# A graph layer with attention, mixer and feed-forward: the one-hots of a lot by four VectorE operations, and ScalarE's weights of a lot ahead of its copy of a finished block

## What is computed

```
xn = layernorm(x)
Wh = xn @ W.T + b                          # 4 heads of 64
e  = leaky_relu(a_src(Wh)[i] + a_dst(Wh)[j], 0.2)
out[i] = sum_j softmax_i(e) * Wh[j]        # the graph part: a sum over the edges of node i
x  = x + out + mix(xn)                     # linear attention, two layer norms, an MLP
x  = x + ffn(layernorm(x))                 # shared MLP and the best 2 of 4 experts
```

## Time and profile before

| | |
|---|---|
| median of 3 runs | 3117.58 us (3114.31 to 3119.29) |
| profiled execution: its own time | 3118.8 us |
| profiled execution: span | 3117.0 us |
| mean granted TensorE clock | 0.847 |
| TensorE busy | 2181.7 us (70%) |
| GpSimd busy | 2160.0 us (69%) |
| VectorE busy | 1882.2 us (60%) |
| ScalarE busy | 792.2 us (25%) |

### The profile page before, as it was taken

How to read it: one execution, slowest core, us unless ns; L and a number is a source line. 1 busy time by engine, 2 the same in 40 slices (tenths; PEclk the granted TensorE clock), 3 DMA queues, 4 the chain that set the end, 5 groups by cost and what they waited for, 6 DMA issues and landing times.

```text
span 3117.0 us, 40701 instructions
## 1 busy us (share of the span) xinstructions
PE 2181.7 (70%) x10817; PEld 1529.3 (49%) x10818; DVE 1882.2 (60%) x3946; ACT 792.2 (25%) x1396; POOL 2160.0 (69%) x2141
## 2 busy tenths in 40 slices
PE   1001984177778787787977879778778787787877
PEld 0000552155555555555655556555555555555554
DVE  8998552265664656666566664656655656666463
ACT  6000442022222222222222222222222222222222
POOL 1008777677777777777777777777777777777770
PEclk6555997588989988989889898889989988989988
DMA  6000221434344444444444444444444444444462
GB/s 188 0 0 13 75 74 41 96 101 119 96 103 124 102 111 116 104 123 103 115 110 104 122 102 124 102 103 123 102 106 124 102 117 108 105 123 103 123 91 29
DMA packets 271584, 306.05 MB, mean 98 GB/s; under 512 B 164258, under 2 KB 210856, under 8 KB 271080
## 3 DMA queue, kind: packets, MB, share of 16 engines
q0 software_dynamic: 97760, 251.60, 30.9%
q1 hardware_dynamic: 140098, 18.08, 3.9%
q10 hardware_dynamic: 33480, 33.36, 3.4%
HBM read 276.25 MB, written 26.62 MB: 97 GB/s over the span
## 4 chain that ended last, share of the span: by engine, by line
PE 50%; DVE 14%; issue 8%; POOL 6%; ACT 2%; DMA 1%; ACTq 0%; DVEq 0%; POOLq 0%; SPq 0%; another core or an unknown queue 0%
PE sum_banks L1027 26%; PE f_banks L1042 9%; POOL gathered L965 6%; DVE onehot L1430 5%; PE turned L999 3%; PE f_banks L1161 2%; DVE gathered L1451 2%; PE f_banks L1086 1%; PE sum_banks L1015 1%; PE f_banks L1067 1%; PE f_banks L1162 1%; DVE he L1579 1%; DVE he L1582 1%; PE f_banks L1068 1%; ACT onehot_t L1202 1%
## 5 line engine op out<-in xcount | busy, mean ns | idle before, releaser
L965 POOL DMA_INDIRECT gathered<-table,col x1872 | 1898.4, 1014 | 572.9 <-issue 563.2
L1027 PE MATMUL sum_banks<-gathered,onehot 128*128 128x260 f32 x3744 | 1070.5, 449 | 105.7 <-DVE gathered L1451 104.4
L1027 PEld LDWEIGHTS sum_banks<-gathered,onehot 128*128 128x128 f32 x3744 | 824.8, 226 | 298.1 <-issue 133.0
L1451 DVE TENSOR_TENSOR gathered<-gathered 128x512 f32<-128x512 f32 x936 | 591.4, 692 | 50.6 <-ACT gathered L1206 47.8
L1430 DVE TENSOR_TENSOR onehot<-iota_row,col 128x1024 f32<-128x1024 f32 x236 | 288.9, 1225 | 448.4 <-PE sum_banks L1027 448.0
L290 POOL DMA_INDIRECT edge_list<-payload,pos x244 | 249.9, 1024 | 293.4 <-DVE pos L411 216.5
L1202 ACT COPY onehot_t<-turned 128x1024 bf16<-128x1024 bf16 x236 | 238.6, 1011 | 332.5 <-PE turned L999 330.2
L1216 ACT COPY acc<-sum_banks x234 | 87.8, 375 | 915.4 <-PE sum_banks L1027 700.0
L999 PE MATMUL turned<-ident_bf,onehot 128*128 128x128 bf16 x1888 | 157.7, 231 | 165.6 <-DVE onehot L1430 165.5
L999 PEld LDWEIGHTS turned<-ident_bf,onehot 128*128 128x128 bf16 x1888 | 115.3, 103 | 183.7 <-DVE onehot L1430 145.6
L1009 PE MATMUL scores<-t,onehot_t 128*128 x1880 | 100.1, 175 | 122.0 <-DVE scored L1439 82.0
(11 more groups left out here) (322 smaller groups left out, 2564.0 us busy)
## 6 DMA issues: line engine op xcount, KB each, us to landing
gathered<-table,col POOLq DMA_INDIRECT x1872
xn_batch<-xn ACTq DMA_DIRECT2D x13, 512.0 KB, 4.3
x_all<-in_x SPq DMA_DIRECT2D x1, 6144.0 KB
x_batch<-in_x ACTq DMA_DIRECT2D x12, 512.0 KB
out<-xf ACTq DMA_DIRECT2D x12, 512.0 KB
edge_list<-xn_all SPq DMA_DIRECT2D x2, 2176.0 KB, 14.1
edge_list<-payload,pos POOLq DMA_INDIRECT x244
col<-edge_list SPq DMA_DIRECT2D x236, 8.0 KB, 2.1
```

Of the source, the lines that this page charges most:

```text
L965: g.indirect_dma_start(gathered[:, l, t, :], None, sh["table"], bass.IndirectOffsetOnAxis(ap=col[l][:, t // G, t % G, 0:1], axis=0)).then_ ...
L1027: last = t.matmul(sum_banks[:, ds(banks_of[g], 1), 0:TB].rearrange("p a w -> p (a w)"), onehot[:, l % 3, g * G + k, :], gathered[:, l, g * ...
L1451: v.tensor_tensor(value, value, gathered[:, l, tiles, C:TB].unsqueeze(3).broadcast_to([P, G, H, HD]), ALU.mult).then_inc(s_mul, 1)
```

## The change

`select` makes the one-hots of a lot by four operations of two tiles (256 elements per partition) each instead of one of eight tiles (1024); the last of them signals `s_sel`. In ScalarE's `lot`, `weights` stands ahead of `block_out`. The rest is the same.

```
--- before.py
+++ after.py
@@ -1216,8 +1216,8 @@
                 s.copy(acc[:, ds(place, 1), :], sum_banks[:, ds(bank, 1), 0:TB]).then_inc(s_cp, 1)
 
             def lot(it, l, piece):
+                weights(it, l)
                 block_out(it, l)
-                weights(it, l)
                 turned_out(*after(it, l, 2))
                 piece(2 * l)
                 piece(2 * l + 1)
@@ -1427,8 +1427,12 @@
                 wait_freed(dve, s_sum, n - 2 if not isinstance(n, int) or n > 2 else 0)
                 dve.wait_ge(s_col[l], 16 * it + 16)
                 within = col[l][:, :, :, :].rearrange("p g k w -> p (g k) w")[:, :, 1:2].bitcast(F32)
-                v.tensor_tensor(onehot[:, l % 3, :, :], iota_row[:, :].unsqueeze(1).broadcast_to([P, TILES, P]),
-                                within.broadcast_to([P, TILES, P]), ALU.is_equal).then_inc(s_sel[l], 1)
+                some = TILES // 4
+                for tiles in (slice(first, first + some) for first in range(0, TILES, some)):
+                    last = v.tensor_tensor(onehot[:, l % 3, tiles, :],
+                                           iota_row[:, :].unsqueeze(1).broadcast_to([P, some, P]),
+                                           within[:, tiles, :].broadcast_to([P, some, P]), ALU.is_equal)
+                last.then_inc(s_sel[l], 1)
 
             def weigh(it, l):
```

## The result

The changed kernel takes 3148.52 us in the median of 4 runs (3144.95 to 3153.18), the kernel before 3118.43 us beside it: ratio 1.0098, 95% interval 1.0080 to 1.0116. It is slower by 30 us. The prediction was 3143 us, slower, with 3113 to 3165 as its range. The profiled execution took 3153.18 us, span 3151.4 us, against 3118.8 and 3117.0 before.

What follows compares the result with a forecast made beforehand. TensorE and VectorE together were taken to bound most lots, the one-hots' end setting the next sums. One-hots at +25 to +35 us, gathers -5, order 0 gave +25 on 3118.8: 3143.8, less 1.2, told as 3143 us; range 3113 to 3165.

Steps and rivals of the forecast that it cites:

- The four operations' time (0.20 us a lot): VectorE's one-hots: four operations instead of one take 0.20 us more per lot, ends 0.16 and 0.46.
- In how many lots (125 to 176): Lots paying the longer one-hots: 125 by their chain share (+25 us), at most 176 where TensorE waits (+35.2 us).
- the lower bound of 125 lots: One-hots' 4.9% of the chain, 153 us, is 125 lots at 1.22 us; at least +25 us is owed.
- The gain from the gathers: GpSimd's gathers stall less beside short one-hot operations: 0.21 us per lot, counted in 22 lots on the chain, -5 us.
- GpSimd's 50 us: GpSimd's time saved: half of 127 us of gather stalls given to the one-hots, four fifths of that goes.
- The sum +25: Whole kernel: middle between 25 - 5 = +20 and 35 - 5 = +30 us, with the weights' order at 0.
- Part 2: Scalar engine's weights ahead of the copy: taken as 0, hidden behind one-hots and TensorE; bounds -18 and +2 us.
- The copy's lateness: Scalar engine's copy now follows exp; only VectorE's L1483 gets later, by 0.23 us in 9 lots: +2 us.
- The gathers decide: Rival: GpSimd's gathers bound the whole stage, so the 50 us are the gain: 3068 us; chance 0.11.
- The weights pay: Rival: TensorE's sums start with exp wherever the product waits for it, -18 us on the path: 3120 us; chance 0.10.
- Short operations pay in full: Rival: VectorE's four one-hot operations don't overlap, 0.46 us more a lot: 3171 to 3194 us; chance 0.10.

Runs made afterwards that it cites:

- the filler: Eight unused identity transposes ahead of TensorE's wait for the one-hots: added to the kernel before 3129.13 us, to the changed kernel 3160.19, to the delay kernel 3151.14.
- the delay kernel: Against the kernel before: one one-hot operation kept, an unread fill of 144 numbers put between it and its signal; 3198.87 us, ratio 1.0261.
- the filled pair: The changed kernel and the delay kernel, each with the filler's eight transposes added: 3160.19 us and 3151.14 us.
- early loads: Against the kernel before, TensorE loads the registers of a lot's sums ahead of the later lot's transposes: 3145.31 us; with the four operations added, 3134.61 us.
- `after`: The changed kernel itself: one-hots by four operations and weights ahead of the copy, against the kernel before; 3148.52 us, ratio 1.0098.

## Why the prediction held, point by point

**The four operations' time (0.20 us a lot)** measured 0.213: a set takes 1.438 us in the mean, and one follows another after (1.43 - 0.42) / 3 = 0.337 us, inside the 0.33 to 0.36 that was said.

The Trainium skill's rule ("VectorE: DVE Perf Modes", section on the TRN2 errata) gave 0.472 us for three more operations of this kind. The trace disagrees for operations back to back: 0.213, and with seven more 0.485 where it gives 1.10.

**In how many lots (125 to 176).** TensorE's added idle time in the changed kernel is 24.5 us. That is what 115 lots give, with the gathers' gain already taken off; the forecast had 25 less 5 to 35 less 5. But the lower bound of 125 lots isn't borne out by the other kernels: 66 and 78 lots with shorter delays, 53 and 61 with the filler, 169 only with the longest. The 57 plain lots pay in full (57 x delay explains what their busy time doesn't); how many of the 119 others pay grows with the delay, from next to none in the delay kernel. So a share in the chain of before was not a debt in as many lots; presumably many have slack that a short delay only uses up, which no run shows by itself.

**The gain from the gathers.** GpSimd's 50 us were 54.7. By cover, counted in the traces: gathers that ran beside one-hot operations took 86 us more than 946 ns each before (430 gathers) and 28 us after (423), two thirds gone; the prediction had 64 and four fifths of it gone.

The Trainium skill ("SBUF — State Buffer", section "Who interferes with whom") says that a VectorE operation with two SBUF inputs contends with a GpSimd instruction that reads SBUF, and that contention for the shared ports is an exclusive lock. The trace agrees for the gathers: beside a one-hot operation of 1.22 us one took 1.59 us in place of 0.946, and ended only 0.83 us after it.

What these 54.7 us were worth was put at -5. VectorE's wait for gathers did fall by 67 us, thirteen times that, yet it is no gain of that size: the delay kernel, whose gathers are no shorter (1017 ns), also has it down to 16.6 us. A slower consumer ends the wait by arriving later. In the filled pair the idle time is that of 61 lots with shorter gathers and of 53 without, a difference of under 2 us, so their worth in this kernel can't be told from nothing.

**The missing term** is the clock. The sum +25 has no term for what TensorE's longer pause does to its own speed. In the plain lots of the changed kernel it is 10.9 us. The other lots had 49 us more at the low level, yet TensorE was busy in them 1.1 us less; the clock's cost there, if any, doesn't show in its work. The page has the same: 9.9 us more busy of 34.4 us more span. So the sum of the terms that the prediction had, 20 to 30, is met by the 24.5 us of idle time, good to some 5 us, and the clock comes on top. (The profiled executions, 34.4 us apart, lie further apart than the medians, 30.1.)

The mechanism was right, and the closeness of the number is in part luck. The clock's term happened to be small for this delay. The same reasoning without it was given for three sister kernels, and missed: by 39 us for the delay of 0.156 us, by 52 for eight operations, by 6 for two, counted from the top of each range. Nothing in the prediction told the changed kernel from the delay kernel in this.

**Part 2** was put at 0, and is 0 within 0.1%. The copy's lateness showed where it was said, at L1483, +2.2 us in its waits with the order alone; in the changed kernel these waits are 13.9 us in 9 places, less than before, so it is too small to be told.

**The rivals.** *The gathers decide* is out in this kernel; in the kernel with early loads, where they are awaited more, the same split saves 10.7 us. *The weights pay* is out by the order alone. *Short operations pay in full* is out by the 0.213.

## What to carry to other kernels

Where TensorE waits for a small operation in each round, that operation's length is paid in each round on the chain; dividing it costs some 0.07 us per further piece here. It paid in two cases: where the waiting engine could start on the first piece and nothing else (here a register load) stood behind it, and beside early loads alone, where gathers are awaited more, though that kernel stayed slower than the one before. Look at the granted clock by stretch before adding a delay of a tenth of a microsecond to TensorE's loop: 0.156 us a lot made TensorE idle 12 us longer in all, and busy 64 us longer with the same work, nearly all of that in plain lots that had been at full clock. And a wait that disappears in the profile isn't a gain until it is shown that the one who waited doesn't merely come later.

## What the runs showed of the hardware

The clock's fall was not expected. A pause of 1.3 us in a lot of 6.4 leaves the plain lots at full clock before, while 0.156 us more in each lot brings 139.9 us at 1.2 GHz into them, and 0.61 us of idle work takes 113 of these back. But it goes not by the pause alone: `after` has the longer delay (0.213) and only 24.4 us at the low level, and the filler leaves 20.5 of those. What differs between the two is open.

Gathers are held in a regular way: of the 229 that take over 1.05 us before, 228 end 0.80 to 0.85 us after the end of a TENSOR_TENSOR operation of VectorE. Not only the one-hots hold them. In the changed kernel one of the longest left (1.86 us, at 1016.86) runs beside a piece's operation of 1024 elements (L1608, 1.22 us).

Eight operations in place of four lengthen the gathers again, to 1046 ns in the mean and 3717 at most, though each operation is shorter (284 ns). The timeline has gathers that get in nowhere:

```profile
1295.14 1.75 DVE L1432 TENSOR_TENSOR onehot<-iota_row,col 128x128 f32<-128x128 f32 x8 [4.76 <-PE sum_banks L1027]
...
1296.81 3.31 POOL L965 DMA_INDIRECT gathered<-table,col  x1 [0.30 <-issue]
1296.82 2.48 DVE L1455 TENSOR_TENSOR gathered<-gathered 128x512 f32<-128x512 f32 x4
```

This one starts with the last one-hot and ends (1300.12) 0.82 us after the fourth product's end (1299.30). In the earlier trace rows a gather got in between the second and the third product. So "a short operation lets the gather in" is not safe: a gather can also be held over a whole row of operations. When it is, no run here settles.
